# A masked attention and expert kernel on one core: division and turning of a batch one step later, low parts on GpSimd in pieces

## What is computed

```python
xn = _layernorm(x)
x = x + attention(xn) + ffn(xn)
# attention: q, k, v = xn @ in_proj; softmax(q k / sqrt(8) + causal mask) @ v; @ out_proj
# ffn: shared(xn) + sum over e of w[e] * expert_e(xn), w from the top 2 of softmax(xn @ wr + rb)
# expert(h) = (silu(h @ g.T) * (h @ u.T)) @ d, inner width 352
```

## Time and profile before

| | |
|---|---|
| median of 3 runs | 471.19 us (468.56 to 472.63) |
| profiled execution | 470.81 us, span in the trace 469.0 us |
| PE busy in the span | 436.3 us (93%) |
| DVE, ACT, POOL busy | 368.5 (79%), 311.4 (66%), 294.2 us (63%) |
| granted TensorE clock, mean | 0.994 |
| attention steps 0 to 63 | about 42.6 to 266 us |
| experts | about 266 to 469 us |

### The profile page before, as it was taken

The page is one execution under the profiler, slowest core; times in us unless marked ns, Lnnn a source line. Parts: engine busy times, 40 slices in busy tenths (PEclk is TensorE's granted clock), DMA queues, the critical chain, the costliest instruction groups (busy, mean ns, idle before and its releaser), DMA issues.

```text
span 469.0 us, 12498 instructions
## 1 busy us (share of the span) xinstructions
PE 436.3 (93%) x3987; PEld 326.2 (70%) x3987; DVE 368.5 (79%) x810; ACT 311.4 (66%) x697; POOL 294.2 (63%) x415
## 2 busy tenths in 40 slices
PE   8978988988999999999888999999999999999995
PEld 4756656655666656666656678888888878888884
DVE  6985999999877887787777177777777888876887
ACT  2636766867677776777777766666767756666652
POOL 1425888888888888888888800447457576575200
PEclk9999899999999999999999999999999999999998
DMA  9786699999875665655539226867968867832762
GB/s 245 226 252 212 185 390 297 306 352 335 284 233 160 170 181 171 172 151 161 160 107 354 60 63 188 263 205 282 330 198 286 293 220 263 270 103 83 230 189 67
DMA packets 60415, 102.00 MB, mean 217 GB/s; under 512 B 11045, under 2 KB 29226, under 8 KB 59328
## 3 DMA queue, kind: packets, MB, share of 16 engines
q1 hardware_dynamic: 55872, 92.74, 62.2%
q0 software_dynamic: 4480, 8.47, 5.4%
HBM read 62.49 MB, written 39.46 MB: 217 GB/s over the span
## 4 chain that ended last, share of the span: by engine, by line
PE 54%; DVE 16%; issue 5%; POOL 5%; ACT 4%; DVEq 0%; POOLq 0%; ACTq 0%
PE ps L823 12%; PE ps L825 11%; PE ps L824 11%; DVE sb_blockmax L1314 7%; PE ps L891 4%; PE ps L952 4%; PE ps L899 3%; PE ps L1117 2%; POOL xs L589 2%; POOL sb_work L613 2%; ACT sb_work L691 2%; PE ps L1106 2%; PE ps L972 1%; PE ps L955 1%; DVE sb_on L1298 1%
## 5 line engine op out<-in xcount | busy, mean ns | idle before, releaser
L1314 DVE TENSOR_REDUCE sb_blockmax<-ps 128x6 f32<-128x768 f32 x128 | 121.7, 956 | 32.0 <-PE ps L899 25.8
L691 ACT ACTIVATE sb_work<-ps 128x768 f32<-128x768 f32 x128 | 104.1, 813 | 53.1 <-PE ps L887 51.8
L634 POOL DMA_INDIRECT ys<-sb_v_all,sb_xn_all x76 | 79.4, 1044 | 75.3 <-DVE sb_v_all L1435 57.0
L613 POOL TENSOR_SCALAR_AFFINE_SELECT sb_work<-sb_work 128x512 f32<-128x512 f32 x128 | 82.8, 649 | 24.2 <-ACT sb_work L691 21.9
L824 PE MATMUL ps<-sb_ring,sb_wb 128*128 128x512 f32 (+1 forms) x231 | 82.8, 358 | 0.0
L589 POOL DMA_INDIRECT xs<-sb_xn_all,sb_posu x64 | 62.9, 983 | 10.7 <-issue 10.7
L1414 DVE TENSOR_TENSOR sb_v_all<-ps,sb_v_all 128x512 f32<-128x512 f32 (+1 forms) x93 | 57.5, 618 | 14.2 <-ACT sb_v_all L771 9.7
L891 PE MATMUL ps<-sb_ring 32*128 32x256 f32 x256 | 49.4, 376 | 11.6 <-ACT sb_work L691 7.2
L771 ACT ACTIVATE sb_v_all<-ps 128x512 f32<-128x512 f32 (+1 forms) x93 | 49.8, 536 | 4.6 <-PE ps L825 3.9
L823 PE MATMUL ps<-sb_ring,sb_wb 128*128 128x512 f32 (+1 forms) x138 | 50.9, 369 | 0.0
L899 PE MATMUL ps<-sb_mask_b,sb_ident_b 128*128 128x256 bf16 x256 | 50.6, 279 | 0.0
(11 more groups left out here) (166 smaller groups left out, 1073.6 us busy)
## 6 DMA issues: line engine op xcount, KB each, us to landing
sb_wb<-wd SPq DMA_DIRECT2D x75, 384.0 KB, 4.0
sb_ring<-qk SPq DMA_DIRECT2D x64, 256.0 KB, 3.6
wd<-sb_wb SPq DMA_DIRECT2D x8, 1152.0 KB, 5.9
xs<-sb_o_all SPq DMA_DIRECT2D x19, 260.0 KB, 3.6
qk<-sb_ring SPq DMA_DIRECT2D x32, 128.0 KB
sb_work<-ys SPq DMA_DIRECT2D x16, 256.0 KB, 3.0
sb_xn_all<-xs SPq DMA_DIRECT2D x15, 260.0 KB, 3.5
sb_o_all<-w SPq DMA_DIRECT2D x8, 384.0 KB, 3.9
```

The costliest lines, as they stand in the source:

```text
L613: pool.affine_select(out=o, in_=o, compare_op=ALU.is_ge, fill=0.0, base=0, pattern=[[0, 4], [1, 128]], channel_multiplier=-1)\
L634: pool.indirect_dma_start(out=ys_d, out_offset=bass.IndirectOffsetOnAxis(ap=row, axis=0), in_=yst[i % NYS][:, EMB * j:EMB * j + EMB], in_o ...
L691: act.activation(part.rearrange("p (k h q) -> p h k q", h=2, q=128), ps[:, 4:6, 0:HEAD].rearrange("p h (k q) -> p h k q", q=128), ACT.Exp, ...
L1314: dve.tensor_reduce(blockmax[:, a:b + 1, 0:3], ps[:, a:b + 1, 0:HEAD].rearrange("p h (k c) -> p h k c", c=128), AX.X, ALU.max).then_inc(s[ ...
```

## The change

Three edits.

1. `scaled(b - 1)` on DVE moves, within the same step `j == 2`, from between the two maxima to behind `negative()`.
2. The two transposes of the batch on PE and ACT's copy of them move from step `j == 2` to step `j == 3` (the new function `turned`); the last batch keeps its place in step 66. Since the half bank is then taken at `j == 3`, the two counts move from steps 7 and 11 to 6 and 10.
3. `attention_low` on GpSimd works in four pieces of 128 columns. The two early ones and the two last ones are four pieces in a row; the four between the scatters are now spread, one piece ahead of each transfer of a tile and behind the wait for that tile's result.

```diff
-        N_COUNT = (7, 11)
+        N_COUNT = (6, 10)
...
+        def turned(n):
+            b, j = quad(n)
+            return b - 1 if j == 3 and isb(b - 1) and isb(b) else NB - 1 if n == NQ + 2 else None
...
-            def attention_low(c):
+            def attention_low(c, j):
+
                 high, low = attention(c)
-                pool.wait_ge(s["oh"], c + 1)
-                pool.tensor_tensor(low, o_all[:, c * TS:(c + 1) * TS], high.bitcast(F32), ALU.subtract)\
-                    .then_inc(s["ol"], 1)
+                part = slice(128 * j, 128 * j + 128)
+                if j == 0:
+                    pool.wait_ge(s["oh"], c + 1)
+                last = pool.tensor_tensor(low[:, part], o_all[:, c * TS + 128 * j:c * TS + 128 * j + 128],
+                                          high[:, part].bitcast(F32), ALU.subtract)
+                if j == SUB - 1:
+                    last.then_inc(s["ol"], 1)
...
             for i in range(NR):
-                if EARLY + i in PARTS:
-                    attention_low(PARTS[EARLY + i])
                 pool.wait_ge(s["yo"], i + 1)
                 for j in range(subs(i)):
+
+                    if EARLY + i in PARTS:
+                        attention_low(PARTS[EARLY + i], j)
...
-                if j == 2 and isb(b - 1):
-                    act.wait_ge(s["tT"], b)
+                c = turned(n)
+                if c is not None:
+                    act.wait_ge(s["tT"], c + 1)
...
-                if j == 2 and isb(b - 1):
-                    pe.wait_ge(s["nm"], b)
+                c = turned(n)
+                if c is not None:
+                    pe.wait_ge(s["nm"], c + 1)
...
                 if isq(m):
                     maximum(0)
-                if j == 2 and 1 <= b < NB:
-                    scaled(b - 1)
...
                 if isq(m) and n >= 0:
                     negative()
+                if j == 2 and 1 <= b < NB:
+                    scaled(b - 1)
```

More of the change, by code:

```diff
@@ L618, in _ @@
                 sends(between, sent(n))
-            def attention_low(c):
+            def attention_low(c, j):
                 high, low = attention(c)
-                pool.wait_ge(s["oh"], c + 1)
-                pool.tensor_tensor(low, o_all[:, c * TS:(c + 1) * TS], high.bitcast(F32), ALU.subtract)\
-                    .then_inc(s["ol"], 1)
+                part = slice(128 * j, 128 * j + 128)
[5 more added lines that the diff above has]
+                    last.then_inc(s["ol"], 1)
             for c in range(EARLY):
-                attention_low(c)
+                for j in range(SUB):
+                    attention_low(c, j)
             for i in range(NR):
-                if EARLY + i in PARTS:
-                    attention_low(PARTS[EARLY + i])
                 pool.wait_ge(s["yo"], i + 1)
                 for j in range(subs(i)):
+                    if EARLY + i in PARTS:
+                        attention_low(PARTS[EARLY + i], j)
                     row = xg[i % NXG][:, j, EMB:EMB + 1].bitcast(U32)
@@ L639, in _ @@
                 if i in PARTS:
-                    attention_low(PARTS[i])
+                    for j in range(SUB):
+                        attention_low(PARTS[i], j)
         @block.scalar
@@ L701, in step @@
                         .then_inc(s["hk" if j else "hq"], 1)
-                if j == 2 and isb(b - 1):
-                    act.wait_ge(s["tT"], b)
-                    if b == 5:
+                c = turned(n)
+                if c is not None:
+                    act.wait_ge(s["tT"], c + 1)
+                    if c == 4:
                         act.wait_ge(s_zero, N_ZERO * 16)
-                    if b == 7:
+                    if c == 6:
                         act.wait_ge(s["wsp"], EXPERTS)
-                    act.activation(o_all[:, (b - 1) * SEQ:b * SEQ], side_out(n), ACT.Copy).then_inc(s["oT"], 1)
+                    act.activation(o_all[:, c * SEQ:(c + 1) * SEQ], side_out(n), ACT.Copy).then_inc(s["oT"], 1)
                 if n in N_COUNT:
@@ L844, in bank_read @@
                     pe.wait_ge(s["lk"], b + 4)
-                if j == 2 and isb(b - 1):
-                    pe.wait_ge(s["oT"], b)
+                if turned(n) is not None:
+                    pe.wait_ge(s["oT"], turned(n) + 1)
                 if n in N_COUNT:
@@ L851, in has_side @@
                 b, j = quad(n)
-                return j in (0, 1) and isb(b + 3) or j == 2 and isb(b - 1) or n in N_COUNT
+                return j in (0, 1) and isb(b + 3) or turned(n) is not None or n in N_COUNT
             def side(n):
@@ L863, in side @@
                         True, True).then_inc(s["pk" if j else "pq"], 1)
-                if j == 2 and isb(b - 1):
-                    pe.wait_ge(s["nm"], b)
+                c = turned(n)
+                if c is not None:
+                    pe.wait_ge(s["nm"], c + 1)
                     for t in range(2):
-                        last = pe.transpose(out[:, 128 * t:128 * t + 128], on[(b - 1) % 2][:, t, :], ident)
+                        last = pe.transpose(out[:, 128 * t:128 * t + 128], on[c % 2][:, t, :], ident)
                     last.then_inc(s["tT"], 1)
```

## The result

The kernel after takes 467.8 us in the median of 14 runs (464.9 to 469.7) where the kernel before takes 470.1 us (468.6 to 474.1): a ratio of 0.9933, with a 95% interval of 0.9908 to 0.9957, that is -3.1 us (-4.3 to -2.0). The forecast was 468.5 us.

What follows compares the result with a forecast made beforehand. It took DVE to bound steps 7 to 22, a loop of waits steps 26 to 61, and PE 283 to 385 us. Terms +0.2 - 1.8 + 0.35 - 1.1 = -2.35 against 470.81 gave 468.5 us, range 466.0 to 471.3.

Steps and rivals of the forecast that it cites:

- Steps 26 to 61: Late attention: eight turnings free 3.0 us of PE waiting, POOL takes part back; -1.8 us, bounds 0 and -3.0.
- End of attention: Last turned batch comes in step 63, so ACT's copy stands before L720 and the silu table load: +0.35 us.
- Expert stage: Low parts in pieces hold DVE's L1421 less, so PE's 1.20 us gap at 386.98 goes: -1.1 us, bounds +2 and -1.2.
- The 0.35 us a meeting: Expert stage: each piece that meets an L1421 holds DVE 0.35 us; two hits a tile against 1.2 us regained.
- The upper bound of 0.77 us: Expert stage: a piece could hold DVE up to 0.77 us, said to follow by scaling 1.63 us held by 1.32 us.
- Steps 0 to 22: Early attention: five turnings with 2.5 us of PE waiting give 0, division under POOL's splitting may lose; +0.2 us, bounds 0 and 0.7.
- The same instructions are done by then: Early steps: the next quad's negative comes at the same time with the division before or behind it, so gain 0.
- DVE sets the time: From 69 to 128 us (steps 7 to 22) DVE is busy 54.58 of 59.00 us and is the bound.
- the counts ... 0: Steps 6 and 10: the moved counts need a choice DVE makes in step 6; DVE is the bound there anyway, 0.
- rival 2: Whole kernel: PE's shifts are swallowed before the next select and its 387 gap only moves; 470.3 to 471.2 us, chance 0.17.
- rival 3: Expert stage: pieces hold DVE 0.77 us a hit, three hits a tile; 471.4 us, or 473 without attention's gain; chance 0.10.
- Rival 1: Attention: POOL and DVE take back less, all 3.0 or even 5.5 us kept; 467.0 us, with all thirteen 464.5; chance 0.15.

Runs made afterwards that it cites:

- e4: The kernel after with the division back between the two maxima, the turning still one step later: 468.1 us, ratio 0.9932.
- e9: The kernel after with whole 128x512 low parts standing where the first piece stands, behind the wait for the tile's result: 467.97 us in one run.
- e8: The kernel after with an extra DVE maximum over 128x384 behind negative() in 32 steps (26 to 57): 486.45 us, where the kernel before took 486.11.
- e11: The kernel after once more, unchanged, on the chip shared with e12: 466.14 us in one run.
- e12: The same edit as e4 once more (kernel after, division back between the maxima), on one chip with e11: 468.56 us in one run.
- e5: The kernel before with each causal select over 128 of its 512 columns: 493.64 us, on a chip where the kernel before took 486.11.
- e6: The kernel after with each causal select over 128 of its 512 columns: 488.91 us, on a chip where the kernel before took 486.11.
- e10: The kernel after with a tile's four pieces in a row ahead of the wait for the tile's result: 468.99 us in one run.
- e1: The kernel before with the low parts in pieces of 128 columns alone: 468.95 us against 471.32, ratio 0.9958.

## Why the prediction was right and where not

**Steps 26 to 61, forecast -1.8, measured -1.85.** Right, and by its steps: PE idle ahead of the turning is gone, the half of step 26 is on its floor, POOL's waiting for ACT fell by 1.8 (about 2 forecast), and the first halves of steps 28, 32, 40 and 48 grew (1.96 to 2.21, 1.71 to 1.88, 1.71 to 1.88, 1.96 to 2.16 us), as did those of 24, 25, 43, 52 and 55, which I hadn't named. The term that sized the gain was the smaller of what a turning frees and of what POOL waits for ACT before the next select that counts. Turning by turning, for steps 26 to 54, what its half gave less what the next halves lost is 0, 0.15, 0.3, 0.4, 0.2, 0.1, 0.3 and 0.2 us, where I had 0, 0.2, 0.4, 0.5, 0.1, 0, 0.3 and 0.2. e4 adds that the turning's move alone gives nearly all of it; e8, that DVE wasn't in it.

**End of attention, forecast +0.35, measured +0.3** (11.2 to 11.5 us from the start of step 62 to the first down projection), with ACT's copy ahead of the table as said.

**Expert stage, forecast -1.1, measured -1.81.** Right in mechanism, a term too small. "I take -1.1 us of the 1.2" priced only the one gap above 0.1 us. By the starts of the down projections the kernel after is ahead by 0.18 us at 382 us, 1.60 at 395 and 1.81 at 407: some 0.6 us more than the gap lay between down projections around the meetings at 385 and 395 us. It stands in no idle time of the rows (PE's adds up to 1.2 us from 283 to 460 us, with ends that are modelled), so I couldn't have read it there, and what PE did in it isn't shown. The 0.35 us a meeting is borne out at its worst (0.34 and 0.33 us at 369.20 and 387.14; 0.26 among the last eight in a row), but only four low parts of these tiles lose anything to speak of, 0.9 us in all, where I had counted two of 0.35 a tile, 2.8. The upper bound of 0.77 us isn't the scaling it is called: 1.63 x 0.457 / 1.32 is 0.56, and 0.77 is the piece plus 0.31. e9 shows besides that the size wasn't the point as such: a whole low part at another place has the same effect.

**Steps 0 to 22, forecast +0.2, measured (over steps 2 to 25) -1.1 in the first profile and +0.55 in e11.** This is the step that failed, in two halves that nearly cancel. "The same instructions are done by then" held for `negative` of the next quad, and missed that of the quad in hand, which comes earlier: in step 14 by 1.3 us from before to after, seen from the start of PE's step 15 (2.28 and 0.94 us behind it). It also took for granted that an instruction lasts as long wherever it stands. Routing pushed behind the division ran under the selects three times as long (0.50 to 1.57 us), and DVE's busy time for the work of steps 9 to 25 falls by 1.2 us from before to after and by 2.3 from e12 to e11 (in e8, on another chip, it doesn't fall). "DVE sets the time" was right for the kernel before, whose DVE waits for PE only 0.2 us in steps 9 to 22, but it left out the next limit: with DMA engines busy at 0.94 of the stretch in the earlier trace rows, an earlier PE waits for its blocks, 1.1 to 4.1 us in the five profiles with division and turning both moved, against at most 0.8 in the four others of the table. Gained 1.0 to 2.4, block waits of 1.1 to 4.1 against it. Net, the timed runs leave -3.1 less the -3.35 of the three late terms, so +0.25 us (-1.0 to +1.4). My sign that I was wrong, steps 0 to 22 shorter, came in one trace and not in the other; the net effect was what I forecast, the reason was not, and that part of the hit is luck. Also "the counts ... 0" holds only because the division went behind the choice: with it ahead (e4, e12) PE waits 1 us more in step 6.

**The sum.** The two profiled spans differ by -3.3 us: +1.4 in steps 0 and 1, where nothing changed and the kernel after happened to have 3.4 us more at half clock, -0.15 before them, -1.1, -1.85, +0.3 and -1.8. Of the rivals, rival 2 falls (both late stretches gained), and rival 3 with it (no meeting above 0.34 us, where it needed about 0.6, and no new gap). Rival 1 was right on the early batches' being worth something, though not by the kept waits it priced.

What stays open: why e5 and e6 stall, what the division's place is worth net (the ratios of e4 and of the kernel after are 0.9932 and 0.9933, but single runs side by side gave 468.56 and 466.14 us), and which transfer makes a block late. In e11 and in the kernel before the block that PE wants in step 9 is asked for 0.7 us after the last store of its batch; PE comes 2.2 us sooner, the load is issued 1.5 us sooner and takes 4.1 us in place of some 3.4. I didn't try to move the loads.

## What to carry to other kernels

Moving a small piece of work behind the instructions that others wait for can pay by its own length, and further by what it no longer pushes into a contended stretch: compare the durations of the same instruction in both orders, not only their places. If an engine's wait is removed, look for who is nearly as late, here POOL's queue in the late steps and the loads in the early ones, and book only the slack that it shows. Where two engines hold each other up, change where they meet before cutting the work to pieces; one of the two is enough.

## What the runs showed of the hardware

A DVE subtraction of two SBUF operands that has started is still held by a GpSimd subtraction that starts 0.44 us later, until 0.56 us behind the latter's end, while GpSimd's takes its usual 1.32 us. One that starts 0.2 us ahead of the end of GpSimd's loses 0.1 us, and one of 128x256 that starts 0.33 us ahead of it 0.2 us (e9). With 128-column pieces in place of the 512 the same meeting costs 0.1 us (e10), but where DVE starts 0.47 us behind GpSimd, four pieces in a row cost 0.7 us, as much as a whole one. The Trainium skill, "SBUF — State Buffer", section "Who interferes with whom", has two-input DVE instructions contend with GpSimd's reads, and tensor_scalar too where it takes both port pairs. The traces agree that they contend: besides the meetings above, the TENSOR_SCALAR on seven columns took 0.60 us under a select and 0.16 without. Which ports it used no run shows.

The granted clock costs this kernel about as much as the change gave. The kernel after in steps 0 and 1, where one stretch at half clock lasts twice as long as in the kernel before:

```profile
45.40:48.80 3.40, 3.40 (x26) 2.33 (x28) 2.32 (x6) 2.46 (x5) 2.62 (x6) 0.50 0.50 155
```

Steps 0 and 1 take 6.80 us without half clock (five profiles), 8.05 with one stretch of 3.4 us (two) and 9.44 with 6.8 us (two): about 1.3 us for each 3.4. It also orders the timed runs. Of the 14 of the kernel after, the five with a mean clock of 0.997 or more took 464.9 to 465.5 us, the nine others, at 0.989 to 0.994, 467.1 to 469.7. Of the 23 of the kernel before beside e1 to e4, ten with 0.996 or more took 469.1 to 470.9, thirteen with less 471.3 to 473.4. One pair of runs can differ by more than the change gave for this reason alone.
